# A recurrent attention kernel: score weight in place of |w3| and sign, one input half on GpSimd, ScalarE's slot 4 in another order

## The reference, cut to what matters

```python
hs = _gru(hist, gru_W, gru_U, gru_b)                      # z, r, tanh candidate
emb = concat([hs, news_b - hs, news_b, hs * news_b])
a = relu(emb @ att_W1 + att_b1)
a = relu(a @ att_W2 + att_b2)
ats = sigmoid(a @ att_W3 + att_b3)                        # one score per row and step
...
def au_step(h, xs):                                       # xu, xr, xc: products of hs
    u = sigmoid(xu_t + h @ au_Uu)
    r = sigmoid(xr_t + h @ au_Ur)
    c = tanh(xc_t + r * (h @ au_Uc))
    u_ = at_t * u
    return (1.0 - u_) * h + u_ * c
...
y = sigmoid(head(concat([h_final, news])))
```

## Time and profile before

| | |
|---|---|
| median of three runs | 1911.28 us (1911.26 to 1912.22) |
| the profiled execution, device time | 1911.32 us |
| its span in the profile | 1909.5 us |
| PE (TensorE) busy | 1893.0 us, 99% of the span |
| GpSimd (POOL) busy | 1636.4 us, 86% |
| VectorE (DVE) busy | 1541.1 us, 81% |
| ScalarE (ACT) busy | 1443.9 us, 76% |
| granted TensorE clock | 1.00 of full speed |

### The profile page before, as it was taken

How to read it: one execution, slowest core, us unless ns; L and a number is a source line. 1 busy time by engine, 2 the same in 40 slices (tenths; PEclk the granted TensorE clock), 3 DMA queues, 4 the chain that set the end, 5 groups by cost and what they waited for, 6 DMA issues and landing times. The chain is left out here.

```text
span 1909.5 us, 46007 instructions
## 1 busy us (share of the span) xinstructions
PE 1893.0 (99%) x17389; PEld 986.4 (52%) x17389; DVE 1541.1 (81%) x2401; ACT 1443.9 (76%) x2470; POOL 1636.4 (86%) x1391
## 2 busy tenths in 40 slices
PE   8999999999999999999999999999999999999998
PEld 4455555555555555555555555555555555555554
DVE  7899988778787877888787778878887877888776
ACT  7778777777777777777777777777777777777775
POOL 7789988888888888888888888888888888888873
PEclk9999999999999999999999999999999999999999
DMA  4211211121121112111211211121112112111100
GB/s 126 79 51 52 73 51 51 51 73 51 51 72 55 51 53 73 51 51 51 73 51 51 68 57 50 56 74 51 51 51 73 51 51 64 60 51 54 65 24 23
DMA packets 50259, 110.65 MB, mean 58 GB/s; under 512 B 16948, under 2 KB 17332, under 8 KB 43704
## 3 DMA queue, kind: packets, MB, share of 16 engines
q1 hardware_dynamic: 49960, 107.99, 17.9%
q10 hardware_dynamic: 144, 0.26, 0.1%
HBM read 107.39 MB, written 0.42 MB: 56 GB/s over the span
## 5 line engine op out<-in xcount | busy, mean ns | idle before, releaser
L1161 PE MATMUL ps<-h_hi,w_hi 128*64 128x512 f16 x1384 | 524.9, 379 | 6.5 <-DVE t L918 3.0
L1162 PE MATMUL ps<-h_hi,w_hi 128*64 128x512 f16 x1384 | 525.0, 379 | 0.0
L1162 PE MATMUL ps<-h_lo,w_hi 128*64 128x512 f16 x1384 | 524.5, 379 | 0.0
L1162 PE MATMUL ps<-h_hi,w_lo 128*64 128x512 f16 x1384 | 524.5, 379 | 0.0
L1161 PE MATMUL ps<-h_lo,w_hi 128*64 128x512 f16 x1384 | 524.5, 379 | 0.0
L1161 PE MATMUL ps<-h_hi,w_lo 128*64 128x512 f16 x1384 | 524.5, 379 | 0.0
L341 POOL TENSOR_TENSOR hn_lo<-hn,hn_hi 128x512 f16<-128x512 f32 x200 | 232.8, 1164 | 143.5 <-ACT hn_hi L483 143.5
L335 POOL TENSOR_TENSOR hn<-h,news 128x512 f32<-128x512 f32 x200 | 255.9, 1280 | 72.0 <-DVE h L1038 71.4
L628 ACT ACTIVATE ps<-gt,p_rest 128x512 f32<-128x512 f32 x185 | 127.7, 690 | 200.8 <-DVE gt L1035 200.8
L354 POOL TENSOR_TENSOR x_lo<-x,x_hi 128x512 f16<-128x512 f32 x196 | 228.8, 1168 | 17.6 <-ACT x_hi L503 13.4
L414 POOL TENSOR_TENSOR d<-h,hc 128x512 f32<-128x512 f32 x186 | 238.3, 1281 | 0.0
(11 more groups left out here) (182 smaller groups left out, 6843.8 us busy)
## 6 DMA issues: line engine op xcount, KB each, us to landing
score<-score_rows SPq DMA_DIRECT2D x50, 1024.0 KB, 4.6
x<-in_xs SPq DMA_DIRECT2D x199, 256.0 KB, 3.1
part_up<-part SPq DMA_DIRECT2D x100, 4.0 KB, 1.8
score_rows<-s_col SPq DMA_DIRECT2D x100, 4.0 KB, 1.4
news<-in_xs SPq DMA_DIRECT2D x4, 256.0 KB, 4.8
p_rest<-in_pack_rest SPq DMA_DIRECT2D x1, 776.0 KB, 6.9
p_att<-in_pack_att SPq DMA_DIRECT2D x1, 290.0 KB, 4.6
x<-in_xs ACTq DMA_DIRECT2D x1, 256.0 KB, 4.0
```

The lines of the kernel that those rows point to most:

```text
L1161: m.matmul(ps[0:H, bank, :], weights[:, 0:H], moving, start=start, stop=stop)
L1162: return m.matmul(ps[H:P, bank, :], weights[:, H:P], moving, start=start, stop=stop)
```

## The change

Three edits. First, the second attention layer's activations: before, the ReLU took a scale |w3| and a bias b2 * |w3| and the step after it multiplied by the sign of w3; now the ReLU takes b2 alone, with no scale operand, and the step after it (`weigh_2`) multiplies by w3. VectorE's five small instructions that made |w3|, the sign and the bias are gone. Second, `input_low(5)` leaves VectorE (where it stood before the first attention sum) and goes to GpSimd; to keep one order for all, GpSimd's `early` now does a slot's input half last, behind the state's halves, and the product `hn` comes ahead of `gated_share`. Third, ScalarE's slot 4 is written out as `first_slot`.

```diff
@@ GpSimd
             def early(low):
-                if low + 2 >= NC + 2:
-                    if low == NC:
-                        pool.wait_ge(xlo_ready, NC + 2)
-                    input_low(low + 2, low + 3)
+                if has(low - 1):
+                    state_news(low - 1, low)
                 if has(low - LAG - 1):
                     gated_share(low - LAG - 1, low - LAG, 16)
                 if has(low - 1):
-                    state_news(low - 1, low)
                     state_low(low - 1, low)
                     state_news_low(low - 1, low)
+                if low + 2 > NC:
+                    if low + 2 == NC + 1:
+                        pool.wait_ge(xlo_ready, NC + 1)
+                    input_low(low + 2, low + 3)
@@ ScalarE
             def relu_2(p, count):
 
                 act.wait_ge(a2_pe[p], count)
-                a.activation(ps[:, B_PAIR[p], :], ps[:, B_PAIR[p], :], ACT.Relu, bias=b_att2[:, 0:1],
-                             scale=w3_col[:, 3:4]).then_inc(a2p_ready[p], NC)
-
-            def sign_2(p, count):
+                a.activation(ps[:, B_PAIR[p], :], ps[:, B_PAIR[p], :], ACT.Relu,
+                             bias=p_att[:, PACK_ATT["b2"]]).then_inc(a2p_ready[p], NC)
+
+            def weigh_2(p, count):
...
-                a.activation(a2[:, p, :], ps[:, B_PAIR[p], :], ACT.Identity, scale=w3_col[:, 2:3]).then_inc(a2_ready[p], NC)
+                a.activation(a2[:, p, :], ps[:, B_PAIR[p], :], ACT.Identity, scale=p_att[:, PACK_ATT["w3"]]).then_inc(a2_ready[p], NC)
...
+            def first_slot():
+                act.wait_ge(r_pe, NC + 1)
+                a.activation(r[:, 0, :], ps[:, B_R, :], ACT.Sigmoid, bias=b_zr[:, 1:2]).then_inc(r_ready, 1)
+                state_news_high(2, 3)
+                second_high(1)
+                state_high(3, 4)
+                relu_1_high(1, 2)
+                act.wait_ge(t2_ready, NC + 1)
+                a.activation(ps[:, B_HC, :], t[:, 0, :], ACT.Tanh, bias=b_h).then_inc(hc_ready, 1)
+                act.wait_ge(z_pe, NC + 1)
+                a.activation(ps[:, B_Z, :], ps[:, B_Z, :], ACT.Sigmoid, bias=b_zr[:, 0:1]).then_inc(z_ready, 1)
+                news_part(3)
+                state_news_high(3, 4)
+                second_high(2)
+                relu_1_high(2, 3)
+                input_high(NC + 3, 32, NC)
@@ VectorE
             input_low(NC)
-            prepare_att_2()
-            input_low(NC + 1)
             dve.wait_ge(c_ready, 1)
             attention_1_news(0, 1)
```

More of the change, by code:

```diff
@@ L139, in rec_kernel @@
         w1_news = sb("w1_news", [P, P])
-        w3_col = sb("w3_col", [P, 4])
-        b_att2 = sb("b_att2", [P, 1])
         ones = sb("ones", [P, P])
@@ L541, in _ @@
             news_part(1)
-            second_high(1)
             news_part(2)
-            state_news_high(2, 3)
             relu_1_high(0, 1)
-            second_high(2)
             def relu_2(p, count):
                 act.wait_ge(a2_pe[p], count)
-                a.activation(ps[:, B_PAIR[p], :], ps[:, B_PAIR[p], :], ACT.Relu, bias=b_att2[:, 0:1],
-                             scale=w3_col[:, 3:4]).then_inc(a2p_ready[p], NC)
-            def sign_2(p, count):
+                a.activation(ps[:, B_PAIR[p], :], ps[:, B_PAIR[p], :], ACT.Relu,
+                             bias=p_att[:, PACK_ATT["b2"]]).then_inc(a2p_ready[p], NC)
+            def weigh_2(p, count):
                 act.wait_ge(a2p_ready[p], count)
@@ L566, in scores_of @@
                 a.activation(s_col[:, :, :], total[:, :, :], ACT.Sigmoid, bias=p_att[:, PACK_ATT["b3"]]).then_inc(s_ready, NC)
+            def first_slot():
[14 more added lines that the diff above has]
+                input_high(NC + 3, 32, NC)
             def early(low):
                 if pairs_of(low - 1):
-                    if low - 1 == TILED:
-                        act.wait_ge(prep, 7)
                     relu_2(0, paired(low - 1))
-                    sign_2(0, paired(low - 1))
+                    weigh_2(0, paired(low - 1))
                 if has(low - LAG - 1):
@@ L581, in early @@
                     relu_2(1, paired(low - 1))
-                    sign_2(1, paired(low - 1))
+                    weigh_2(1, paired(low - 1))
                 if has(low - LAG):
@@ L585, in early @@
                     a.activation(gu[:, (low - LAG) % 2, :], ps[:, B_GU, :], ACT.Sigmoid, bias=b_gated[:, 0:1]).then_inc(gu_ready, 1)
[L586 to L591, removed]
+                state_news_high(low - 1, low)
+                relu_1_high(low - 2, low - 1)
                 if folds_of(low):
@@ L597, in early @@
                 a.activation(ps[:, B_Z, :], ps[:, B_Z, :], ACT.Sigmoid, bias=b_zr[:, 0:1]).then_inc(z_ready, 1)
-                if low == NC:
-                    state_news_high(3, 4)
-                    relu_1_high(2, 3)
                 if has(low - LAG - 3):
@@ L620, in slot @@
                     relu_2(0, paired(s0 + (off - 1)))
-                    sign_2(0, paired(s0 + (off - 1)))
+                    weigh_2(0, paired(s0 + (off - 1)))
                 if has(low - LAG - 1):
@@ L632, in slot @@
                     relu_2(1, paired(s0 + (off - 1)))
-                    sign_2(1, paired(s0 + (off - 1)))
+                    weigh_2(1, paired(s0 + (off - 1)))
                 if has(low):
@@ L668, in slot @@
                     a.activation(d1_hi, w_d1[:, :], ACT.Copy).then_inc(d1_half, 1)
-            for s in range(NC, EARLY):
+            first_slot()
+            for s in range(NC + 1, EARLY):
                 early(s)
@@ L706, in late @@
                     relu_2(0, ITEMS)
-                    sign_2(0, ITEMS)
+                    weigh_2(0, ITEMS)
                 act.wait_ge(gt2_ready, item - NC)
@@ L713, in late @@
                     relu_2(1, ITEMS)
-                    sign_2(1, ITEMS)
+                    weigh_2(1, ITEMS)
                 if has(low - 2):
@@ L787, in split_att_low @@
                 v.tensor_tensor(att_lo, att_w, att_hi, ALU.subtract).then_inc(att_split, 1)
[L789 to L798, removed]
             def sum_2(p, count):
```

## The result

The changed kernel took 1908.06 us in the median of 17 runs (1907.52 to 1909.33), the kernel before, on the same chip, 1911.94 (17 runs, 1910.86 to 1912.67). The profiled execution took 1908.02 us, 3.30 less than the profiled one before.

A forecast was written before the change was run, and what follows sets the result against it. TensorE, busy almost throughout from 120 to 1880 us, bounds the kernel, so only its waits can move. From 1911.32 us, -3.88 - 0.3 - 0.4 + 0.85 + 0.98 = -2.75 gives 1908.6 us, range 1906.6 to 1910.0.

The forecast's parts named there:

- Slot 4 and 5: r of slot 4 starts 3.31 us earlier, so TensorE's start in attention_2(1) of slot 5 comes 3.88 us earlier.
- `hn` freed and the weight split: hn no longer waits for the input half in slots 7 and 9, weight split freer in 8 and 12: 0.3 us gained.
- The ReLU: ReLU without scale, two per slot in slots 6, 10 and 14, 0.06 us each, at most some 0.10: 0.4 us gained.
- up to 0.2: ReLU's possible gain in the last ten slots, where TensorE waits for gate gu; left out of the sum.
- `gus` behind `hn`: Score product behind hn delays VectorE's gated_step and through t TensorE: losses of 0.85 us in slot 11, 0.98 in slot 13.
- the 0.08 that it took off in slot 11: Some 0.08 us comes back where VectorE's weight split finds GpSimd idle, leaving slot 11's loss at 0.85 us.
- Slot 12: Later score product costs nothing, since VectorE's 32-column sum waits for GpSimd anyway; by the port lock nothing is gained either.
- rival B: The wait for the score product is paid in slot 12 too, another 0.95 us lost: 1909.5 us; chance 0.12.
- C: Slower: r of slot 4 doesn't start early; at its old start the sum is +0.56, 1911.9 us; chance 0.04.
- D: Gain of slots 4 and 5 is taken back before slot 9 by the vector side's own bound: 1910.8 us; chance 0.06.
- A: The later score product costs nothing, TensorE or VectorE having slack in slots 11 and 13: 1906.7 us; chance 0.22.

The follow-up runs named there:

- e4: The kernel before with the first edit alone (plain ReLU, w3 in the step behind it, VectorE's five small instructions gone); 1908.93 us, ratio to before 0.9986.
- e9: The kernel before with the new activations but VectorE's five small instructions kept, their results unused; 1911.03 us, ratio to before 0.9995.
- e3: The changed kernel with ScalarE's slot 4 in the order of before, the other edits kept; 1909.16 us, ratio to before 0.9988.
- e8: The changed kernel with the score product ahead of hn and GpSimd's input half first in the slot again from slot 6; 1906.28 us, ratio to before 0.9969.
- e1: The changed kernel with the score product ahead of hn again in slots 11 to 13; 1906.12 us, ratio to before 0.9970.
- e2: The changed kernel with a scale operand of ones at the second attention layer's ReLU; 1908.65 us, ratio to before 0.9985.
- e7: The kernel before, unchanged, profiled once more; 1912.05 us, ratio 1.0000.
- e6: The changed kernel with six unused one-column VectorE instructions added at the start; 1908.04 us, ratio to before 0.9980.
- e5: The changed kernel with the score product ahead of hn and VectorE's 32-column sum behind t's first step in slots 8 and 12; 1904.63 us, ratio 0.9963.

## Why the prediction was right, and where it was short

**Slot 4 and 5 (forecast -3.88): right, row by row.** r at 21.38 (21.40), `hn_hi` of item 2 at 21.96 (21.97), the five GpSimd steps at the very starts that were forecast, the wait for `hn_lo` 0.18 (0.15), `attention_2(1)` at 32.68 (32.68). In distances it is 3.83. The runs split it: the five instructions 1.61 of it (e4 at slot 5, where the ReLU has no part yet by e9), the input half and ScalarE's order 2.22 together, and of the order 1.16 if the rest is there (e3). No run moves the input half alone, so its own share stays open. Stepping through the engine that is the slower one, by starts, was enough; durations would not have been, since neighbours overlap.

**`hn` freed and the weight split (forecast -0.3): 0.40** between e8 and e1.

**The ReLU (forecast -0.4): 0.49** (e9 against before) or 0.51 (e2 against after) up to slot 15, the same in two surroundings. The prediction took 0.06 each from the step behind the ReLU, which has one pointer and lasts 0.69, and named 0.10 as the upper bound. The bound was the right value: the ReLU with one pointer lasts 0.66, and the step behind it starts 0.10 us earlier, counted from the ReLU's start. The Trainium skill (ScalarE: Activation LUTs, "ACT is a hardware spline evaluator", under "What ACT_TABLE_LOAD costs") gives about 93 ns for each pointer operand; these rows agree with 0.10. In the tail it gave 0.19, the "up to 0.2" that the prediction left out of its sum.

**`gus` behind `hn` (forecast +0.85 and +0.98): 1.02 and 1.07** (e1). VectorE's waits of 1.06 and 1.10, less the 0.03 or 0.04 that stands before this step anyway, come whole to TensorE. The forecast of the losses was short by 0.17 and 0.09, for two reasons. It gave at most 0.05 us to the handover from h to `hn` and 0.04 to that from `gus` to `gated_step`, which took 0.08 and 0.10. And the 0.08 that it took off in slot 11 for the weight split does not belong there: the split does get shorter (0.55 for 0.70), but e1, where `gus` stands first, has that too (74.94, 0.55 us), so that it is part of the 0.40 above. The prediction had also named one way to TensorE only, through t. There is a second, through the gated state g, and in slot 13 TensorE waited for it first (87.30, 1.00 us) and for t after it (88.58). That changed no number, since both stand behind the same `gated_step`.

**Slot 12 (forecast: nothing gained, nothing lost): right.** e1 and after take the same 7.24 us from slot 12's start behind t to slot 13's, and VectorE's `gated_step` of slot 12 stands idle for 0.04 us only (77.52). That also ended rival B. C fell with r at 21.38, D with the gain of slot 5 still whole at slot 9 (4.28 in distances), A with e1.

**What the sum missed.** By slot 15 the distances give -3.83 - 0.40 - 0.5 + 2.10, which is -2.63 for a measured -2.66, where the forecast had -2.75. So the terms before the steady loop were right to about 0.1 in sum; singly they missed by 0.05 to 0.17, and cancelled in part: the gains of `hn` and of the ReLU were put too low, and so were both losses. Three things behind or ahead of them are missing, which the sum had at nothing: the first the prediction named and left out, the other two it did not have. One is the ReLU in the tail, 0.19. One is the tail gap, 0.39. TensorE waited at 1870.17 for the gate gu; VectorE's rows of before:

```profile
1866.92 0.68 DVE L1132 TENSOR_TENSOR gt<-gr,ps 128x512 f32<-128x512 f32 x1
1868.10 0.69 DVE L1136 TENSOR_TENSOR gt<-gt,ps 128x512 f32<-128x512 f32 x1 [0.50 <-DVE gt L1132]
```

and of after:

```profile
1864.02 0.68 DVE L1124 TENSOR_TENSOR gt<-gr,ps 128x512 f32<-128x512 f32 x1
1864.81 0.69 DVE L1128 TENSOR_TENSOR gt<-gt,ps 128x512 f32<-128x512 f32 x1
```

The second step starts 1.18 us behind the first where 0.79 is its pace, and nothing that the trace shows holds it: the queue's wait before it is over at 1867.64, 0.46 us ahead of its start (0.07 in after), GpSimd runs the same `g_lo` beside it in both kernels, and the nearest transfers of instructions start at 1860.21 and 1870.96. This extra 0.39 is there in before, e7 and e9, which have the five small instructions, and absent in the eight kernels that don't. It is not the ReLU (e2, e9), and a shift of VectorE's stream by six instructions does not bring it back (e6). What does it in those three was not found, and stays open. With it, 2.66 + 0.19 + 0.39 is 3.24, the whole of the profiles' 3.30 but for the start.

The last is the start phase, 3.88 between the medians less 3.24: about 0.6 us. The working: device time of the profiled execution less its reset start is 1890.34 for before and 1887.09 for after. If the rest of the program is as constant as the distances are, the medians put that start at 21.6 in before and 21.0 in after; e7 and e9 come to 21.8 and 21.4, the seven others without the five instructions to 20.8 to 21.1. It looks as if the five also lengthen the start phase in the typical run, but no pair of profiles shows how, and the start phase also moves with a thing that differs from execution to execution (the last section). This is argued, not shown.

That the forecast time of 1908.6 lies within 0.5 us of the measured 1908.06 is in part luck. The gain was 3.88 where 2.75 was forecast, 1.1 us more; but the forecast started from an execution of before (1911.32) that was 0.6 us faster than before's median in the 17 runs (1911.94), which cancels more than half of the miss.

Of the 3.24 us, then: the ReLU 0.49 and 0.19, the five instructions 1.48 (in the surroundings of before) and the tail's 0.39, which comes and goes with them, less 2.10 for the score product behind `hn`. What is left over, 2.79, goes to the input half and ScalarE's order (with the half last on GpSimd, 0.40 of it); it is a remainder and not a measurement.

## What to carry to other kernels

When an engine's program is reordered for the sake of one slot, read what the same code does in the slots where the other work stands between: here one order for all slots gave back 2.1 of 5.3 us, and e1 shows that it needn't. Where TensorE is saturated later on, only the starts in the fill count, and a forecast by stepping through the slower engine's starts, slot by slot, was good to about 0.1 us in sum and 0.17 in a single term. Place a small VectorE sum of two SBUF tiles behind the step that others wait for, not ahead of it, if GpSimd is at work then (e5: 1.3 us for moving two instructions).

## What the runs showed of the hardware that I had not expected

An instruction on a single column isn't always short on VectorE: of the five in before, two took 0.99 and 1.20 us (19.19 and 20.21) because they ended only with GpSimd's instruction beside them, two of the same size took 0.15 and 0.14.

The first fp32 matmuls of TensorE last about 1.1 us in some executions and 0.64 to 0.66 in others. Before and after:

```profile
4.93 1.12 PE L1161 MATMUL ps<-x,p_gru 128*64 128x512 f32 x1 [0.44 <-DMA p_gru<-in_pack_gru]
```

```profile
5.14 0.64 PE L1153 MATMUL ps<-x,p_gru 128*64 128x512 f32 x1 [0.64 <-DMA p_gru<-in_pack_gru]
```

Before, e7, e1, e3, e8 and e9 are of the first kind, after, e2, e4, e5, e6 of the second, so the kernel's code does not decide it: e1 and e2 differ from after by a few instructions that come much later. In the first kind pairs start about every 0.85 us at first, as in e7 from 6.94 to 7.79, and then every 0.43. The traces show what changes then: their records of the granted clock begin there, at full speed (2.4 GHz), at 7.27 us in before, 10.62 in e7, 9.86 in e1, 6.13 in e3, 7.08 in e8 and 7.31 in e9, and at 4.31 to 4.97 in the five of the second kind, ahead of the first of these matmuls or, in e5, 0.08 us behind its start. A mean clock of 1.00 that a view gives for a stretch ahead of the first record is no measurement. Half the pace fits the lower level, 1.2 GHz, though no record of this stretch says so. In all eleven TensorE ran seven matmuls from 1.33 to 4.50 us, one every 0.43 us, and then waited for a DMA.

When the clock comes late it sets the start phase: the reset's last pair starts at 22.41 in e1 and 22.77 in e7, and at 20.38 to 20.98 in the nine where full speed is on record by 7.31. So two profiles of one code differ by 1.8 us there (before and e7), and the eleven by 2.4. A gain of 1 us behind the start phase is read by distances; one inside it can't be read from a single pair of profiles.
